# A decoder stack in fp32: weights repacked by the host, and the first tile's GpSimd and VectorE work in another order

## The chip, the cores and the metric

The kernel runs on one core of one Trainium2 chip. The metric is the device time of one execution in microseconds (us), lower is better. Before the change three executions took 3156.26, 3157.49 and 3159.41 us, a median of 3157.49 us. The engines in what follows: TensorE (PE; PEld is its weight load), VectorE (DVE), ScalarE (ACT), GpSimd (POOL), and SyncE (SP), which here only issues DMAs.

## The reference, cut to what matters

A stream x of 16 sequences of 128 tokens with 256 features passes three blocks, each on a normalised x and added to it. The change touches the first, a stack of 8 layers of linear attention and a feed-forward part.

```python
x = x + _L0_attn_ref(_layernorm(x, axis=-1), Wq, bq, Wk, bk, Wv, bv, Wo, bo, ln1_s, ln1_b, W1, b1, W2, b2, ln2_s, ln2_b)
x = x + _L0_xattn_ref(_layernorm(x, axis=-1), ctx_512, ...)
x = x + _L0_ffn_ref(_layernorm(x, axis=-1), ...)

def _L0_attn_ref(x, ...):                      # B, H, D, K, F = (8, 16, 256, 64, 1024)
    for i in range(B):
        residual = x
        Q = _feature_map(jnp.einsum('nsd,hdk->nshk', x, Wq[i]) + bq[i])      # elu(.) + 1
        Kf = _feature_map(jnp.einsum('nsd,hdk->nshk', x, Wk[i]) + bk[i])
        V = jnp.einsum('nsd,hdk->nshk', x, Wv[i]) + bv[i]
        KV = jnp.sum(Kf * V, axis=1)
        sumK = jnp.sum(Kf, axis=1)
        Z = 1.0 / (Q * sumK[:, None] + 1e-06)
        att = (Q * KV[:, None] * Z).reshape(n, s, H * K)
        y = jax.nn.gelu(att @ Wo[i] + bo[i])
        x = _layer_norm(y + residual, ln1_s[i], ln1_b[i])
        residual = x
        h = jax.nn.gelu(x @ W1[i] + b1[i])
        h = jax.nn.gelu(h @ W2[i] + b2[i])
        x = _layer_norm(h + residual, ln2_s[i], ln2_b[i])
    return x
```

## The kernel before, in words

The 16 sequences are four tiles of four sequences (512 tokens); x stays in SBUF as X. A layer's 16 heads are eight chunks of two heads, worked on in four pairs of chunks, p = 0 to 3. The stack is written as slots: slot(l, t) does the late parts of tile t (output projection, feed-forward) beside the projections and the attention of tile t+1. slot(0, -1) is the opening: only the four pairs of tile 0, with nothing else for TensorE to do. slot(0, 0) and slot(0, 1) follow, and then a loop over the layers. Each engine runs its own list of instructions in the order written, and semaphores join them. There is no scheduler.

**Weights.** An fp32 product is made of three fp32r products, so each weight is split into a high and a low part on GpSimd: `split_piece` waits for the piece in one of three STAGE buffers (`staged`), makes the high part (L262) and the low part (L264), and counts it in `w_lo`. A layer has 12 pieces: eight of 768 columns (Wk, Wv, Wq of two heads, 384 KB) and four of 512 columns (W1, 256 KB). SyncE loads piece k once `w_lo` says that piece k-3 is split. TensorE's pair p of tile 0 waits for `w_lo` of 2p+2 pieces.

**The input's norm.** For tile t, VectorE makes the statistics (L787, L791), GpSimd the rstd (L269, L271), VectorE the normed X (L779, four instructions, counted in `x0`). For tile 0, TensorE transposes X into PSUM (L375), ScalarE rounds it to XTHI (L550), and VectorE makes the remainder XTLO (L692). Only then can the projections start.

**One pair.** TensorE makes K, Q and V of two chunks, 36 matmuls (L341 to L343). ScalarE clips K (L505) and Q (L513) and takes Exp of both at once (L517). VectorE: `features` (L635, then L641 for K and L645 for Q, which read and free the PSUM banks that TensorE's next pair waits for), `sums_of` (L655, L660), `denominators` (L667, L669, L673, L676, L679). ScalarE then inverts (`invert`, L525 and L527), and VectorE's `newton` (L685, L687) corrects the inverse. ScalarE's `weigh` (L540) makes the attention from it. ScalarE's own order in slot(0, -1) puts `invert` of pair p-1 between the clips of K and of Q of pair p; the inversion of pair 2 stands behind the Exp of pair 3. EX and INV have two buffers each, so pair p+2 waits for pair p.

VectorE's order before: all statistics and all four norms of the input come first (L779 of tiles 1 to 3 before any `features`); GpSimd's order has rstd(t) in front of the pieces 2t and 2t+1. Tiles 1 to 3 of the normed input are first read in slots (0, -1) (tile 1, at its end), (0, 0) and (0, 1).

## Time and profile before

| what | value |
|---|---|
| median of three runs | 3157.49 us (3156.26 to 3159.41) |
| profiled execution, its time | 3159.65 us |
| its span, first to last instruction | 3158.1 us |
| mean granted TensorE clock | 0.963 |
| TensorE busy | 2933.1 us, 93% |
| VectorE busy | 2325.5 us, 74% |
| ScalarE, GpSimd busy | 1862.7 us, 921.5 us |
| DMA | 92.90 MB, mean 29 GB/s, 210193 packets, of them 147056 under 512 B |
| TensorE busy from 0 to 20, 20 to 45, 45 to 80 us | 1.97, 11.41, 25.88 us |
| TensorE busy from 200 to 300 us | 99.62 us |

Read the last two lines first: TensorE is close to full in the steady part of the stack and nearly empty in the first 80 us.

### The profile page before, as it was taken

Reading aid. Unit: us, or ns where it says so; the run is one execution under the profiler, and the core shown is the slowest. Engines: PE = TensorE matmul, PEld = TensorE weight load, DVE = VectorE, ACT = ScalarE, POOL = GpSimd, SP = SyncE. Lnnn points to the kernel's source line nnn. Section 1 sums busy time; section 2 is a strip of 40 time slices with the busy share of each in tenths; the row PEclk is TensorE's granted clock in tenths of the full one; section 3 lists DMA queues with packets and bytes.
Section 4 is the critical chain, followed back from the end, with each engine's and each line's share of the span. In section 5 each row is a group of like instructions: output and inputs, shape, how many; then the busy total and the mean of one; then the engine's idle time right before and its main releaser. Section 6 shows DMA issues by size and latency. Waiting matters only on the chain. (4 is left out here: it accounts for less than half of the span.)

```text
span 3158.1 us, 35422 instructions
## 1 busy us (share of the span) xinstructions
PE 2933.1 (93%) x11342; PEld 1989.8 (63%) x11343; DVE 2325.5 (74%) x3334; ACT 1862.7 (59%) x2796; POOL 921.5 (29%) x590
## 2 busy tenths in 40 slices
PE   4799999999999999999999999999999977997995
PEld 3566666666666665666566656665666635775563
DVE  7778888888887888887878788879787826763111
ACT  3666676667666776777677767776777713441121
POOL 5004231423152315231513151315131133333002
PEclk8899999999999999999999999999999987996998
DMA  5001101110111001100110011001100008000012
GB/s 129 1 1 23 26 8 32 27 27 6 30 27 27 12 25 27 27 17 19 26 27 17 19 26 27 17 19 26 28 17 4 1 3 269 0 0 24 12 45 77
DMA packets 210193, 92.90 MB, mean 29 GB/s; under 512 B 147056, under 2 KB 203632, under 8 KB 210000
## 3 DMA queue, kind: packets, MB, share of 16 engines
q1 hardware_dynamic: 207360, 83.30, 10.2%
q0 software_dynamic: 2640, 7.21, 0.7%
q8 instruction: 99, 1.62, 0.2%
q14 instruction: 94, 0.77, 0.1%
HBM read 80.24 MB, written 10.22 MB: 29 GB/s over the span
## 5 line engine op out<-in xcount | busy, mean ns | idle before, releaser
L341 PE MATMUL PS<-XTHI,WHI 128*128 128x512 f32 x1536 | 655.5, 427 | 60.8 <-DVE EX L641 41.5
L342 PE MATMUL PS<-XTLO,WHI 128*128 128x512 f32 x1536 | 614.1, 400 | 0.0
L343 PE MATMUL PS<-XTHI,WLO 128*128 128x512 f32 x1536 | 613.6, 399 | 0.0
L269 POOL TENSOR_TENSOR RSTD<-MV,EPS 128x4 f32<-128x4 f32 x68 | 41.1, 605 | 1537.7 <-DVE MV L713 1529.8
L391 PE MATMUL Y<-H,W2S 128*128 128x512 f32 x1024 | 458.2, 596 | 2.7 <-DVE R L703 2.7
L391 PE MATMUL Y<-ATT,WO 128*128 128x512 f32 x1024 | 451.7, 594 | 4.1 <-ACT ATT L540 2.7
L540 ACT ACTIVATE ATT<-INV,CC,CE 128x128 f32<-128x128 f32 x1024 | 424.9, 481 | 3.7 <-DVE INV L687 3.7
L341 PEld LDWEIGHTS PS<-XTHI,WHI 128*128 128x128 f32 x1536 | 294.5, 192 | 153.6 <-issue 64.6
L505 ACT ACTIVATE EX<-PS,BNEG 128x512 f32<-128x512 f32 x256 | 169.8, 686 | 309.9 <-PE PS L343 307.6
L342 PEld LDWEIGHTS PS<-XTLO,WHI 128*128 128x128 f32 x1536 | 294.8, 192 | 83.6 <-issue 20.3
L343 PEld LDWEIGHTS PS<-XTHI,WLO 128*128 128x128 f32 x1536 | 294.0, 191 | 70.0
L391 PEld LDWEIGHTS Y<-ATT,WO 128*128 128x128 f32 x1024 | 194.7, 190 | 226.2 <-issue 215.2
L391 PEld LDWEIGHTS Y<-H,W2S 128*128 128x128 f32 x1024 | 192.9, 191 | 210.9 <-issue 202.5
L660 DVE TENSOR_REDUCE SUMS<-EX 128x16 f32<-128x2048 f32 x128 | 292.4, 2284 | 3.3
L635 DVE TENSOR_SCALAR EX<-EX 128x2048 f32<-128x2048 f32 x128 | 224.2, 1752 | 43.1 <-ACT EX L517 43.0
L517 ACT ACTIVATE EX<-EX 128x2048 f32<-128x2048 f32 x128 | 245.3, 1917 | 4.1
L673 DVE TENSOR_TENSOR EX<-EX,ES 128x1024 f32<-128x1024 f32 x128 | 234.2, 1830 | 5.5
L685 DVE TENSOR_TENSOR EX<-EX,INV 128x1024 f32<-128x1024 f32 x128 | 164.8, 1287 | 90.5 <-ACT INV L527 90.2
L566 ACT ACTIVATE H<-PS,B 128x512 f32<-128x512 f32 x256 | 176.7, 690 | 79.7 <-PE PS L343 79.7
L341 PE MATMUL PS<-X1HI,W1HI 128*128 128x512 f32 x512 | 206.2, 403 | 0.1
L342 PE MATMUL PS<-X1LO,W1HI 128*128 128x512 f32 x512 | 203.1, 397 | 0.0
L703 DVE TENSOR_TENSOR R<-Y,R 128x1024 f32<-128x1024 f32 x32 | 39.2, 1225 | 222.3 <-PE Y L384 222.3
(180 smaller groups left out, 4823.9 us busy)
## 6 DMA issues: line engine op xcount, KB each, us to landing
STAGE<-L_attn_Wk SPq DMA_DIRECT2D x128, 64.0 KB, 2.1
STAGE<-L_attn_Wv SPq DMA_DIRECT2D x128, 64.0 KB, 2.1
STAGE<-L_attn_Wq SPq DMA_DIRECT2D x128, 64.0 KB, 2.1
WO<-L_attn_Wo SPq DMA_DIRECT2D x8, 1024.0 KB, 5.5
W2S<-L_attn_W SPq DMA_DIRECT2D x8, 1024.0 KB, 5.6
STAGE<-L_attn_W SPq DMA_DIRECT2D x64, 128.0 KB, 3.7
WGU<-L_ffn_r_gate SPq DMA_DIRECT2D x8, 512.0 KB, 10.2
WGU<-L_ffn_r_up SPq DMA_DIRECT2D x8, 512.0 KB, 9.5
```

The source lines that it names most:

```text
L341: nc.tensor.matmul(out, whi[:, kc, :], xhi[:, kc, :], start=(kc == 0), stop=False)
L342: nc.tensor.matmul(out, whi[:, kc, :], xlo[:, kc, :], start=False, stop=False)
L343: ins = nc.tensor.matmul(out, wlo[:, kc, :], xhi[:, kc, :], start=False, stop=(kc == KD - 1))
L391: ins = nc.tensor.matmul(Yfm[:, m, :], w[:, c, m * P:(m + 1) * P], src[:, c, :], start=(c == 0), stop=(c == HC - 1))
L505: nc.scalar.activation(EX[:, b, 2 + i, :], PS[:, KB + i, :], ACT.Relu, scale=-1.0, bias=BNEG[:, 0, 2 * p + i:2 * p + i + 1])
L517: nc.scalar.activation(EX[:, b, 2:6, :], EX[:, b, 2:6, :], ACT.Exp, scale=-1.0).then_inc(ex, 1)
L540: ins = nc.scalar.activation(ATT[:, 2 * p + i, ss], INV[:, b, i, ss], ACT.Identity, scale=CE[:, b, k:k + 1], bias=CC[:, b, k:k + 1])
L566: nc.scalar.activation(H[:, m, :], PS[:, QB + m % 4, :], ACT.Gelu_apprx_tanh, bias=B1[:, m:m + 1]).then_inc(h_act, 1)
L635: nc.vector.tensor_scalar(EX[:, b, 2:6, :], EX[:, b, 2:6, :], -1.0, 1.0, ALU.add, ALU.add).then_inc(snap, 1)
L660: nc.vector.tensor_reduce(SUMS[:, b, :], by_seq(EX[:, b, 0:4, :]), AX.X, ALU.add).then_inc(sums, 1)
L673: nc.vector.tensor_tensor(q, q, spread(ES[:, b, :], SEQ), ALU.add).then_inc(denom, 1)
L685: nc.vector.tensor_tensor(EX[:, b, 4:6, :], EX[:, b, 4:6, :], INV[:, b, :, :], ALU.mult).then_inc(residue, 1)
```

## The change

Host side: a function `packed` rearranges the stack's weights before launch, so that each SBUF tile or staged piece is one run of memory per partition in DRAM. Kernel side, the loads become one DMA each: a piece of Wk, Wv and Wq is one DMA with rows of 3 KB in place of six DMAs with rows of 256 B; a W1 piece one in place of two; the K, V and Q biases of half a layer one in place of three. Wo, W2 and the biases bo, b1, b2 keep their one DMA each, from the new layout. The semaphore counts follow. The splits stay the same.

In the opening, VectorE's order changes: XTLO of tile 0 comes right behind the norm of tile 0, and the norms of tiles 1, 2 and 3 move behind `denominators` of pairs 0, 1 and 2, in front of `newton`. `slot(0, -1)` is written out as a loop, in which every pair ends with its own `newton` before the next pair's `features`; before, `features` of pair 3 stood in front of `newton` of pair 2. GpSimd makes the rstd of tiles 1 to 3 together in front of piece 2, and waits for the normed X of tile 0 (`x0`) before it splits piece 0.

```diff
         def piece_incs(k):
-            return 16 * (3 * KD if k < HC else 2)
+            return 16
...
                 if k < HC:
-                    for m, w in enumerate((Wk, Wv, Wq)):
-                        dst = STAGE[:, s, m * KD * P:(m + 1) * KD * P]
-                        for kc in range(KD):
-                            src = w[layer, 2 * k:2 * k + 2, kc * P:(kc + 1) * P, :].rearrange("h p k -> p h k")
-                            sp.dma_start(dst[:, kc * P:(kc + 1) * P].rearrange("p (h k) -> p h k", h=2),
-                                         src).then_inc(staged[s], 16)
+                    sp.dma_start(STAGE[:, s, :], Wkvq[layer, k, :, :]).then_inc(staged[s], 16)
                 else:
...
+                    sp.dma_start(STAGE[:, s, 0:2 * KD * P], W1[layer, k - HC, :, :]).then_inc(staged[s], 16)
...
             def load_fm(dst, b, layer, done):
-                sp.dma_start(dst[:, :], b[layer, :].rearrange("(c p) -> p c", p=P),
-                             allow_slow_non_contiguous=True).then_inc(done, 16)
+                sp.dma_start(dst[:, :], b[layer, :, :]).then_inc(done, 16)
...
             for k in range(HC):
-                if k % 2 == 0:
-                    t = k // 2
-                    bs = slice(t * TS, (t + 1) * TS)
-                    rstd(RSTD0[:, bs], MV0[:, bs, 1], EPS0, mv0, 2 * t + 2, r0, t + 1)
+                if k == 0 or k == 2:
+                    for t in range(TILES)[:1] if k == 0 else range(1, TILES):
+                        bs = slice(t * TS, (t + 1) * TS)
+                        rstd(RSTD0[:, bs], MV0[:, bs, 1], EPS0, mv0, 2 * t + 2, r0, t + 1)
+                if k == 0:
+
+                    pool.wait_ge(x0, 1)
                 split_piece(0, k, True)
...
             input_statistics(0)
             norm_input(0)
+            input_lo(0)
             input_statistics(1)
-            input_lo(0)
             input_statistics(2)
             input_statistics(3)
-            for t in range(1, TILES):
-                norm_input(t)
-            slot(0, -1)
+            for p in range(PAIRS):
+                features(0, 0, p)
+                sums_of(0, 0, p)
+                denominators(0, 0, p)
+                if p < TILES - 1:
+                    norm_input(p + 1)
+                if p < PAIRS - 1:
+                    newton(0, 0, p)
+            input_lo(1)
             slot(0, 0)
```

VectorE at the start, before: BN_STATS and BN_AGGR are the statistics, `X<-X,MV,RSTD` the norm, and the last row the first instruction of pair 0.

```order
L779 TENSOR_SCALAR X<-X,MV,RSTD 128x256 x4
L787 BN_STATS ST<-X 128x6 x4
L791 BN_AGGR MV<-ST 128x2 x4
L692 TENSOR_TENSOR XTLO<-PS,XTHI 128x1024
L787 BN_STATS ST<-X 128x6 x4
L791 BN_AGGR MV<-ST 128x2 x4
L787 BN_STATS ST<-X 128x6 x4
L791 BN_AGGR MV<-ST 128x2 x4
L779 TENSOR_SCALAR X<-X,MV,RSTD 128x256 x12
L635 TENSOR_SCALAR EX<-EX 128x2048
```

VectorE at the start in the changed kernel (its line numbers are lower by ten: L769 is L779 before, L682 is L692, L625 is L635):

```order
L769 TENSOR_SCALAR X<-X,MV,RSTD 128x256 x4
L682 TENSOR_TENSOR XTLO<-PS,XTHI 128x1024
L777 BN_STATS ST<-X 128x6 x4
L781 BN_AGGR MV<-ST 128x2 x4
L777 BN_STATS ST<-X 128x6 x4
L781 BN_AGGR MV<-ST 128x2 x4
L777 BN_STATS ST<-X 128x6 x4
L781 BN_AGGR MV<-ST 128x2 x4
L625 TENSOR_SCALAR EX<-EX 128x2048
```

The twelve norm instructions of tiles 1 to 3 are gone from the front of pair 0, and XTLO stands ahead of the statistics of tile 1.

VectorE from the end of pair 0 to the start of pair 1, before: L660 is the reduce of `sums_of`, L667 to L679 are `denominators`, L685 and L687 are `newton`.

```order
L660 TENSOR_REDUCE SUMS<-EX 128x16
L667 TENSOR_SCALAR SUMS<-SUMS 128x8
L669 RECIPROCAL ES<-SUMS 128x8
L673 TENSOR_TENSOR EX<-EX,ES 128x1024
L676 SCALAR_TENSOR_TENSOR CC<-SUMS,ES 128x8
L679 TENSOR_TENSOR CE<-CC,ES 128x8
L685 TENSOR_TENSOR EX<-EX,INV 128x1024
L687 SCALAR_TENSOR_TENSOR INV<-EX,INV 128x1024
L635 TENSOR_SCALAR EX<-EX 128x2048
```

The same place in the changed kernel:

```order
L650 TENSOR_REDUCE SUMS<-EX 128x16
L657 TENSOR_SCALAR SUMS<-SUMS 128x8
L659 RECIPROCAL ES<-SUMS 128x8
L663 TENSOR_TENSOR EX<-EX,ES 128x1024
L666 SCALAR_TENSOR_TENSOR CC<-SUMS,ES 128x8
L669 TENSOR_TENSOR CE<-CC,ES 128x8
L769 TENSOR_SCALAR X<-X,MV,RSTD 128x256 x4
L675 TENSOR_TENSOR EX<-EX,INV 128x1024
L677 SCALAR_TENSOR_TENSOR INV<-EX,INV 128x1024
L625 TENSOR_SCALAR EX<-EX 128x2048
```

Four norm instructions (L769) stand between `denominators` and `newton`; four more each stand at that place of pairs 1 and 2.

GpSimd up to piece 3 before, where `WHI` and `WLO` are the two halves of one piece's split and `RSTD` the rstd of one tile:

```order
L271 TENSOR_TENSOR RSTD<-RSTD,HALF 128x4
L262 TENSOR_TENSOR WHI<-STAGE,ONE 128x768
L264 TENSOR_TENSOR WLO<-STAGE,WHI 128x768
L262 TENSOR_TENSOR WHI<-STAGE,ONE 128x768
L264 TENSOR_TENSOR WLO<-STAGE,WHI 128x768
L269 TENSOR_TENSOR RSTD<-MV,EPS 128x4
L271 TENSOR_TENSOR RSTD<-RSTD,HALF 128x4
L262 TENSOR_TENSOR WHI<-STAGE,ONE 128x768
L264 TENSOR_TENSOR WLO<-STAGE,WHI 128x768
```

And in the changed kernel:

```order
L251 TENSOR_TENSOR WLO<-STAGE,WHI 128x768
L256 TENSOR_TENSOR RSTD<-MV,EPS 128x4
L258 TENSOR_TENSOR RSTD<-RSTD,HALF 128x4
L256 TENSOR_TENSOR RSTD<-MV,EPS 128x4
L258 TENSOR_TENSOR RSTD<-RSTD,HALF 128x4
L256 TENSOR_TENSOR RSTD<-MV,EPS 128x4
L258 TENSOR_TENSOR RSTD<-RSTD,HALF 128x4
L249 TENSOR_TENSOR WHI<-STAGE,ONE 128x768
```

Three rstds stand ahead of piece 2, and none later: the pieces 2 to 11 follow one another.

## Rows read from the trace of the kernel before

**Rows 1.** The page's busy times, then the waits from 0 to 200 us.

```profile
PE 2933.1 (93%) x11342; PEld 1989.8 (63%) x11343; DVE 2325.5 (74%) x3334; ACT 1862.7 (59%) x2796; POOL 921.5 (29%) x590
...
PE PS L341 <- DVE EX L641: 26.7, 4, 13.8
```

**Rows 2.** The tile STAGE from 200 to 2500 us: waits for it.

```profile
  PE PS L343: 7.1, 7
```

**Rows 3.** Timeline, 7 to 25 us: start, us, engine, instruction, [idle before].

```profile
9.03 1.46 POOL L262 TENSOR_TENSOR WHI<-STAGE,ONE 128x768 fp32r<-128x768 f32 x1
9.07 4.09 DVE L779 TENSOR_SCALAR X<-X,MV,RSTD 128x256 f32<-128x256 f32 x4 [1.51 <-POOL RSTD L271]
...
15.22 1.01 ACT L550 CAST XTHI<-PS 128x1024 fp32r<-128x1024 f32 x1 [11.80 <-PE PS L375]
...
17.57 1.40 DVE L787 BATCH_NORM_STATS2 ST<-X 128x6 f32<-128x256 f32 x4 [4.41 <-DMA X<-x]
...
19.30 1.19 DVE L692 TENSOR_TENSOR XTLO<-PS,XTHI 128x1024 fp32r<-128x1024 f32 x1
...
20.60 0.77 PE L341 MATMUL PS<-XTHI,WHI 128*128 128x512 f32 x1 [5.41 <-DVE XTLO L692]
20.73 1.47 POOL L262 TENSOR_TENSOR WHI<-STAGE,ONE 128x768 fp32r<-128x768 f32 x1
...
24.05 1.52 POOL L262 TENSOR_TENSOR WHI<-STAGE,ONE 128x768 fp32r<-128x768 f32 x1
```

**Rows 4.** Line L779 from 9 to 14 us: ns min/median/max.

```profile
L779 DVE TENSOR_SCALAR X<-X,MV,RSTD x4: 400/984/1952, 9.1 to 12.8; 128x256 f32<-128x256 f32 x4
```

**Rows 5.** Timeline, 28 to 32 us.

```profile
28.84 6.82 DVE L779 TENSOR_SCALAR X<-X,MV,RSTD 128x256 f32<-128x256 f32 x4 [0.90 <-POOL RSTD L271]
...
29.97 1.92 ACT L517 ACTIVATE EX<-EX 128x2048 f32<-128x2048 f32 x1
```

**Rows 6.** Timeline, 43 to 61 us, VectorE alone.

```profile
43.54 1.21 DVE L635 TENSOR_SCALAR EX<-EX 128x2048 f32<-128x2048 f32 x1
...
48.94 2.29 DVE L660 TENSOR_REDUCE SUMS<-EX 128x16 f32<-128x2048 f32 x1
...
51.78 1.23 DVE L673 TENSOR_TENSOR EX<-EX,ES 128x1024 f32<-128x1024 f32 x1
52.92 1.00 DVE L676 SCALAR_TENSOR_TENSOR CC<-SUMS,ES 128x8 f32<-128x8 f32 x1
...
55.22 1.23 DVE L685 TENSOR_TENSOR EX<-EX,INV 128x1024 f32<-128x1024 f32 x1 [1.10 <-ACT INV L527]
56.48 1.95 DVE L687 SCALAR_TENSOR_TENSOR INV<-EX,INV 128x1024 f32<-128x1024 f32 x1
58.35 2.28 DVE L635 TENSOR_SCALAR EX<-EX 128x2048 f32<-128x2048 f32 x1
```

**Rows 7.** Timeline, 52 to 58 us, GpSimd alone.

```profile
52.10 1.80 POOL L262 TENSOR_TENSOR W1HI<-STAGE,ONE 128x512 fp32r<-128x512 f32 x1 [8.63 <-DMA STAGE<-L_attn_W]
53.98 1.31 POOL L264 TENSOR_TENSOR W1LO<-STAGE,W1HI 128x512 fp32r<-128x512 f32 x1
```

**Rows 8.** Timeline of SyncE's DMA issues; then all packets from 32 to 56 us.

```profile
35.16 0.47 SPq L192 DMA_DIRECT2D WO<-L_attn_Wo  x1
...
DMA packets 7510, 3.83 MB, mean 159 GB/s; under 512 B 3412, under 2 KB 7508, under 8 KB 7508
```

**Rows 9.** Timeline, 84 to 99 us, pair 3 and the start of slot (0, 0).

```profile
84.89 1.23 DVE L635 TENSOR_SCALAR EX<-EX 128x2048 f32<-128x2048 f32 x1 [1.00 <-ACT EX L517]
...
85.83 1.06 ACT L527 ACTIVATE INV<-INV 128x1024 f32<-128x1024 f32 x1
...
96.87 1.22 DVE L692 TENSOR_TENSOR XTLO<-PS,XTHI 128x1024 fp32r<-128x1024 f32 x1
...
98.19 0.77 PE L341 MATMUL PS<-XTHI,WHI 128*128 128x512 f32 x1 [9.09 <-issue]
```

**Rows 10.** Windows: length, busy (instructions) of PE, PEld, DVE, ACT, POOL; PEclk, DMA.

```profile
80.00:120.00 40.00, 28.27 (x103) 19.90 (x102) 28.42 (x37) 24.44 (x37) 0.00 (x0) 0.83 0.00 1
```

More of the change, by code:

```diff
@@ L162, in load_piece @@
                 if k < HC:
[L163 to L175 removed]
+                    sp.dma_start(STAGE[:, s, :], Wkvq[layer, k, :, :]).then_inc(staged[s], 16)
+                else:
+                    sp.dma_start(STAGE[:, s, 0:2 * KD * P], W1[layer, k - HC, :, :]).then_inc(staged[s], 16)
             def load_ba(layer, half):
                 cs = slice(half * HC // 2, (half + 1) * HC // 2)
[L179 to L181 removed]
+                sp.dma_start(BA[:, :, cs], bkvq[layer, half, :, :, :]).then_inc(ba_in[half], 16)
             def load_ln(dst, scale, bias, layer, done):
@@ L187, in load_fm @@
             def load_fm(dst, b, layer, done):
-                sp.dma_start(dst[:, :], b[layer, :].rearrange("(c p) -> p c", p=P),
-                             allow_slow_non_contiguous=True).then_inc(done, 16)
+                sp.dma_start(dst[:, :], b[layer, :, :]).then_inc(done, 16)
             def load_wide(dst, w, layer, done):
-                sp.dma_start(dst[:, :, :], w[layer, :, :].rearrange("(c p) n -> p c n", p=P)).then_inc(done, 16)
+                sp.dma_start(dst[:, :, :], w[layer, :, :, :]).then_inc(done, 16)
             def layer_loads(l):
@@ L494, in clip_keys @@
                     cs = slice(2 * p, 2 * p + 4)
[L495 removed]
+                    act.wait_ge(ba_in[p // 2], (l + 1) * 16)
                     if at_least(l, t, 1):
@@ L1720, in decoder, with packed, by_side @@
             mixture(nc, X, ident, out, ffn)
+def packed(a, np):
+    out = {n: v for n, v in a.items() if n[:8] != "L0_attn_"}
+    def by_side(w, sizes):
+        return np.ascontiguousarray(w.reshape(sizes[0]).transpose(sizes[1]).reshape(sizes[2]))
+    L = LAYERS
+    w = [a["L0_attn_W" + n].reshape(L, HC, 2, KD, P, HK) for n in "kvq"]
+    out["L0_attn_Wkvq"] = by_side(np.stack(w, 2), ((L, HC, 3, 2, KD, P, HK), (0, 1, 5, 2, 4, 3, 6), (L, HC, P, PIECE)))
+    b = [a["L0_attn_b" + n].reshape(L, 2, HC // 2, P) for n in "kvq"]
+    out["L0_attn_bkvq"] = by_side(np.stack(b, 2), ((L, 2, 3, HC // 2, P), (0, 1, 4, 2, 3), (L, 2, P, 3, HC // 2)))
+    out["L0_attn_W1"] = by_side(a["L0_attn_W1"], ((L, KD, P, HC // 2, 2, P), (0, 3, 2, 4, 1, 5), (L, HC // 2, P, 2 * KD * P)))
+    for n in ("Wo", "W2"):
+        out["L0_attn_" + n] = by_side(a["L0_attn_" + n], ((L, HC, P, D), (0, 2, 1, 3), (L, P, HC, D)))
+    for n, c in (("bo", KD), ("b1", HC), ("b2", KD)):
+        out["L0_attn_" + n] = by_side(a["L0_attn_" + n], ((L, c, P), (0, 2, 1), (L, P, c)))
+    for n in ("ln1_s", "ln1_b", "ln2_s", "ln2_b"):
+        out["L0_attn_" + n] = a["L0_attn_" + n]
+    return out
 def kernel(**inputs):
@@ L1730 @@
               for name, a in inputs.items()}
+    arrays = packed(arrays, np)
     aps = {name: nc.dram_tensor(name, a.shape, mybir.dt.from_np(a.dtype), kind="ExternalInput").ap()
```

14 lines of the change are left out of this document (2 added, 12 removed).

## The prediction

> **What bounds the kernel now.** First the page's busy times and the waits from 0 to 200 us [rows 1]. TensorE is busy 2933.1 of 3158.1 us, and its largest wait of the first 200 us has one place: 13.8 of the 26.7 us that it waited for VectorE's L641. Then the loop over the layers. Of its STAGE buffers the one wait that shows is for TensorE to free the weights, 7.1 us in 7 [rows 2], and none is for a DMA. So in the loop the weights are there before GpSimd wants them, and whatever the new loads save there is worth nothing. What is left is the opening, and there I read the timeline.
>
> TensorE starts the projections at 20.60, when XTLO is done [rows 3]. XTLO itself ran at 19.30 though its input was ready at 16.23 (15.22 + 1.01): VectorE stood in its list at the statistics of tile 1, whose X landed at 17.57. ScalarE's Exp of pair 0 ends at 31.89 (29.97 + 1.92) [rows 5], but `features` starts at 43.54 [rows 6], since the norms of tiles 2 and 3 stand in front. One set of four takes 6.82 us [rows 5] where a lone instruction takes 0.40 [rows 4]: VectorE gets one instruction in per instruction of GpSimd. So 11.65 us are lost between Exp and `features`, and TensorE, whose PSUM banks are freed by `features`, waits with it.
>
> How VectorE and GpSimd exclude each other carries most of the sum. Row L676 took 1.00 us at 52.92 to the end of GpSimd's high part (52.10 + 1.80); that one in its turn took 1.80, since it had waited for L673 to end at 53.01 [rows 6, 7]. VectorE's L687 (1.95), and L635 (2.28 against 1.21), show the same. XTLO and the reduce L660 have no second length beside GpSimd in these rows, and I take the same of L641, L645 and L655, which read PSUM as XTLO does. The Trainium skill, "SBUF — State Buffer", section "Who interferes with whom", says that an instruction with two SBUF inputs or in a two-port mode and a GpSimd instruction block each other whole. If the port were shared in bandwidth instead, step 3 below would cost next to nothing and the light rival would be the forecast; by that rule, it would not.
>
> **The change part by part**, against the profiled execution (3159.65 us, its span 3158.1 plus 1.5, and 2.2 above the median of 3157.49). I give times as they would stand in a trace.
>
> 1. Start. The rstd of tile 0 ends at 9.03 as now. GpSimd now waits for the norm, so it runs alone: four at a pitch of 0.34 (0.40 each, overlapping; the pitch is an estimate from the length and the 0.06 that follows it) end at about 10.45, not 13.16. That brings the transposes, XTHI (16.23 now, so 13.5) and XTLO (14.8) 2.7 us and more forward. GpSimd's first two pieces start at 10.5 instead of 9.03, and a piece takes 3.32 (20.73 to 24.05) [rows 3], so w_lo reaches 2 at 10.5 + 6.7 = 17.2. Their data must be there: six issues a piece become one, and X and three pieces are requested in about 4 us. TensorE starts at 17.25 instead of 20.60: 3.35 us.
>
> 2. `features` of pair 0. Exp ended 11.3 us after TensorE's start (31.89 - 20.60), so it ends at 28.55, and VectorE is free: three statistics of about 1.75 from 14.8 end at 20.1. `features` can start at 28.55 instead of 43.54: 15.0 us.
>
> 3. What comes back. GpSimd used to be idle from 43.5 to 52.10, the 8.63 us of waiting for W1 [rows 7]; pair 0 ran in that hole. Now GpSimd makes three rstds and starts piece 2 at about 21.6. Six pieces of 3.32 last to 41.5 even undisturbed, then W1's four pieces of 2.4 (1.04 when not blocked, 1.31, and gaps). Pair 0 meets that train. Walking down VectorE's list: L635 meets a high part begun at 28.45, waits to 29.95 and ends at 31.05. L641 to L660 are not touched and take 6.4 (51.23 - 43.54 less the 1.25 of L635) to 37.45. L667 waits for a high part (37.85), L673 for the low part behind it, done 40.75; L676 and L679 for another high part, 42.5. The first instruction of the norm of tile 1 waits for the last low part of the pieces, 44.1, and ends at 44.45. Whether the other three cost 1.05 or one W1 instruction each (1.2) hangs on when W1's first piece lands. Wo was requested at 35.16 [rows 8], and W1 was there at 52.10, 17 us later, behind 2.6 MB and the biases in 4-byte elements. Now Wo goes at 33.4, when piece 7 may be loaded (w_lo of 5), and without the single elements: an estimate of 11 to 13 us puts it at 44.5 to 46.5. I take 45.4. Then the norm ends at 45.5, L685 waits for one W1 instruction (47.7), L687 and the next L635 for one each, and this L635, of pair 1, ends at 52.25. It ended at 60.63 before. So from 15.0 ahead VectorE falls to 8.4 ahead: step 3 costs 6.6. Behind it GpSimd is through with W1 at about 58.4, before L667 of pair 1, and the norm of tile 2 stands where VectorE waits for ScalarE's inversion anyway. The bounds: 0, without any blocking, even a gain of 1.1, since L635, L676 and L687 were blocked before; and 9.1, if W1 is there at 44.1 and all three norm instructions, L685, L687 and L635 take a W1 instruction each.
>
> 4. Pair 3. `features` stood ahead of `newton` of pair 2 and started at 84.89. Now `newton` comes first and needs ScalarE's inversion, which stands behind the Exp of pair 3 and ends at 86.89 (85.83 + 1.06) [rows 9]. From there VectorE's list holds the same instructions as before up to XTLO of tile 1, 13.2 us (84.89 to 98.09), with no wait among them, and TensorE starts slot (0, 0) behind that XTLO, 0.1 us later (98.19). So 2.0 us are lost. The norm of tile 3 (1.4) hides in the wait. Bounds: 0, if the inversion came in time, and 2.4, were `newton` wholly added.
>
> 5. The rest. The loads in the loop: 0 [rows 2], below nothing excluded and above nothing too, since none is waited for. After slot (0, 0) has begun, each engine's list is unchanged, so what is gained there stays.
>
> Sum: -15.0 + 6.6 + 2.0 = -6.4 us, a span of 3151.7 and 3151.1 against the median. I say **3151.3 us**.
>
> The Trainium skill, "DMA: Bandwidth & Descriptors", section "Rules for kernel authors", says that a last dimension that isn't contiguous costs one descriptor an element. The trace agrees in that 3412 of 7510 packets were under 512 B between 32 and 56 us [rows 8]; some 1536 of them would be these biases. By that rule alone the queue in front of W1 empties sooner than I took it, which makes the dense train below likelier and not the forecast better.
>
> **The rivals.**
>
> Dense train. W1 lands before GpSimd is free at 44.1, or X so late (as at 17.57 now) that the whole train moves back and covers more of pair 1. GpSimd then has no hole, and VectorE gets one instruction in per GpSimd instruction through norm and `newton`. For: four norm instructions took 6.82 in such a train [rows 5]. Against: W1 took 17 us to come before. Step 3 costs 9.1 instead of 6.6: -3.9, 3153.6 us. With a late X 1 to 2 more.
>
> Light train. VectorE reaches its blocked instructions in GpSimd's gaps, or W1 comes after 47. For: a tie of 0.1 us decides at 28.5, worth 1.3, and L676 found GpSimd's gap between 53.90 and 53.98 [rows 6, 7]. Against: GpSimd is busy without a hole until 44. With W1 late -7.9 (3149.6); with no blocking at all -15.0 - 1.1 + 2.0 = -14.1 (3143.4).
>
> Given back later. TensorE in slots (0, 0) to (0, 2) waits for something not moved by the opening, so part of the gain ends in a wait there. For: no row that I have. Against: Wo was requested at 35.16 [rows 8] and is used after 98. It would be worth 2 to 6 us of the gain: 3153 to 3157.
>
> Slower, by TensorE's clock. From 80 to 120 us the granted clock is 0.83 at 28.27 us of work [rows 10], so part of slot (0, 0) runs at the lower of its two levels after stretches of waiting, as the start does too. If the moved waits left it all at 1.2 GHz, this work would take (0.83 - 0.5) / 0.5 of 28.27 longer, 18.7 us, and the time would be 3169.8 us. It ends on the slow side once more than 12.7 us are lost so, that is if that stretch falls below about 0.61. For: TensorE still waits between pairs. Against: it waits less than before ahead of pair 1 and of slot (0, 0).
>
> That the change doesn't do what it says: only if TensorE's pair 1 waits for the pieces 2 and 3, split by 28.4, needed at 31.8. Three us of delay in X would start it, and each more costs its length; it is part of the dense train.
>
> **How the numbers follow.** Forecast case (W1 within some 1.5 us of GpSimd's being free, -4.8 to -8.4): 0.43. Dense train 0.23, light train 0.22, given back 0.06, slower by the clock 0.06. A change of this kernel's time by under 0.2%, 6.3 us, can hardly be told from none. The forecast case straddles that bound, half on each side. Faster: 0.21 + 0.22 = 0.43. Within: 0.22 + 0.23 + 0.06 = 0.51. Slower: 0.06. The range from 3145.5 to 3157.0 leaves out the no-blocking end and the clock, and holds the others; the forecast case alone spans 3149.1 to 3152.7.
>
> **What the changed profile would show.** Step 1: the four norms in under 1.6 us, TensorE's L341 at 17.3, waiting for GpSimd's `w_lo` and no longer for XTLO. Step 2: L635 of pair 0 at 28.6. Step 3: L673, L676 and the norm of tile 1 stretched to GpSimd's pitch, and L635 of pair 1 done at 52.3; W1's high part waiting little or not at all for its DMA. Step 4: VectorE waiting for ScalarE's L527 ahead of `newton` of pair 2, about 2 us. Step 5: TensorE's slot (0, 0) starts near 91.8, and from there each engine's later rows lie 6.4 us earlier. I am wrong if pair 1's L635 ends outside 50 to 55.5, if slot (0, 0) starts as forecast and the span doesn't follow, or if the stretches after 200 us have other busy shares.

## The result and the profile after

The changed kernel takes **3142.58 us** (median of five runs, 3137.61 to 3144.07), the kernel before 3157.49 us (3155.34 to 3159.41): a ratio of 0.995, with an interval of 0.9936 to 0.9965. The gain of 14.9 us is more than twice the 6.4 us forecast, and the time lies below the range given (3145.5 to 3157.0). The profiled execution is the 3142.58 us one, with a span of 3140.5 us.

The page of the changed kernel, which answers [rows 1]:

```profile
PE 2925.5 (93%) x11342; PEld 1984.7 (63%) x11343; DVE 2305.1 (73%) x3334; ACT 1863.0 (59%) x2796; POOL 922.0 (29%) x590
...
DMA packets 59658, 92.82 MB, mean 30 GB/s; under 512 B 14960, under 2 KB 38768, under 8 KB 57424
```

The same bytes go in 59658 packets, where it was 210193. The waits from 0 to 200 us (total, times, longest):

```profile
PE PS L331 <- DVE EX L631: 22.5, 4, 9.5
```

TensorE's longest wait for `features` fell from 13.8 to 9.5 us. The waits for STAGE buffers between 200 and 2500 us still name no DMA [rows 2]:

```profile
  PE PS L333: 12.2, 7
```

The timeline of the start (start, us, engine, instruction, idle before and its releaser), against [rows 3]:

```profile
9.02 1.38 DVE L769 TENSOR_SCALAR X<-X,MV,RSTD 128x256 f32<-128x256 f32 x4 [1.51 <-POOL RSTD L258]
...
12.46 1.01 ACT L540 CAST XTHI<-PS 128x1024 fp32r<-128x1024 f32 x1 [9.03 <-PE PS L365]
...
13.50 1.23 DVE L682 TENSOR_TENSOR XTLO<-PS,XTHI 128x1024 fp32r<-128x1024 f32 x1 [3.10 <-ACT XTHI L540]
...
17.28 0.77 PE L331 MATMUL PS<-XTHI,WHI 128*128 128x512 f32 x1 [4.86 <-POOL WLO L251]
...
26.43 1.92 ACT L507 ACTIVATE EX<-EX 128x2048 f32<-128x2048 f32 x1
...
28.38 2.08 DVE L625 TENSOR_SCALAR EX<-EX 128x2048 f32<-128x2048 f32 x1 [8.52 <-ACT EX L507]
```

VectorE from `denominators` of pair 0 on, against [rows 6]:

```profile
37.48 2.45 DVE L663 TENSOR_TENSOR EX<-EX,ES 128x1024 f32<-128x1024 f32 x1
39.86 1.43 DVE L666 SCALAR_TENSOR_TENSOR CC<-SUMS,ES 128x8 f32<-128x8 f32 x1
...
41.40 2.88 DVE L769 TENSOR_SCALAR X<-X,MV,RSTD 128x256 f32<-128x256 f32 x4
44.20 1.21 DVE L675 TENSOR_TENSOR EX<-EX,INV 128x1024 f32<-128x1024 f32 x1
45.45 1.23 DVE L677 SCALAR_TENSOR_TENSOR INV<-EX,INV 128x1024 f32<-128x1024 f32 x1
46.59 2.06 DVE L625 TENSOR_SCALAR EX<-EX 128x2048 f32<-128x2048 f32 x1
...
55.88 2.09 DVE L663 TENSOR_TENSOR EX<-EX,ES 128x1024 f32<-128x1024 f32 x1
```

GpSimd beside it, against [rows 7]:

```profile
41.34 1.82 POOL L251 TENSOR_TENSOR WLO<-STAGE,WHI 128x768 fp32r<-128x768 f32 x1
45.97 1.61 POOL L249 TENSOR_TENSOR W1HI<-STAGE,ONE 128x512 fp32r<-128x512 f32 x1 [2.80 <-DMA STAGE<-L_attn_W]
```

GpSimd is through with the pieces at 43.16 and has nothing until W1's piece is there at 45.97. Into that hole fall the end of the norm and both halves of `newton`: L675 and L677 take 1.21 and 1.23 us, their length with no GpSimd beside them.

Pair 3 and the start of slot (0, 0), against [rows 9]:

```profile
65.51 0.76 PE L331 MATMUL PS<-XTHI,WHI 128*128 128x512 f32 x1 [5.46 <-DVE EX L631]
...
77.36 1.06 ACT L517 ACTIVATE INV<-INV 128x1024 f32<-128x1024 f32 x1
78.45 1.23 DVE L675 TENSOR_TENSOR EX<-EX,INV 128x1024 f32<-128x1024 f32 x1 [4.12 <-ACT INV L517]
...
90.44 1.22 DVE L682 TENSOR_TENSOR XTLO<-PS,XTHI 128x1024 fp32r<-128x1024 f32 x1
...
91.75 0.77 PE L331 MATMUL PS<-XTHI,WHI 128*128 128x512 f32 x1 [6.21 <-issue]
```

Slot (0, 0) starts at 91.75, 6.44 us ahead of 98.19. The window after it has the clock it had [rows 10]:

```profile
80.00:120.00 40.00, 30.21 (x104) 20.77 (x105) 28.41 (x36) 21.69 (x32) 0.00 (x0) 0.83 0.00 1
```

**Where the rest came from.** As a mark in every slot I take the first multiply of the first layer norm on GpSimd (one a tile, 32 in all). Its first stands at 148.96 before and 142.21 after, its last at 2550.51 and 2536.73: 6.75 us ahead at the loop's start, 13.78 at its end. So the loop over the layers, where I had said nothing changes, gave 7.0 us. What follows the last mark (607.6 and 603.8 us) isn't different in kind: over all profiles here it is 598 to 613 us. By slots, 5.5 of the 7.0 us lie in six of them, those that begin with the loop's return. One row differs there on every return: the pause of ScalarE ahead of its table load. Kernel before, its waits, then the timeline of the fourth return:

```profile
ACT L546 <- issue: 15.2, 6, 2.7
```

```profile
1507.01 1.28 ACT L546 ACT_TABLE_LOAD   x1 [2.46 <-issue]
...
1510.49 1.23 DVE L685 TENSOR_TENSOR EX<-EX,INV 128x1024 f32<-128x1024 f32 x1 [3.05 <-ACT INV L527]
```

Changed kernel, the same two views:

```profile
ACT L536 <- issue: 9.4, 6, 1.8
```

```profile
1499.16 1.28 ACT L536 ACT_TABLE_LOAD   x1 [1.45 <-issue]
...
1502.64 1.23 DVE L675 TENSOR_TENSOR EX<-EX,INV 128x1024 f32<-128x1024 f32 x1 [2.04 <-ACT INV L517]
```

The table load waits for nothing that the profile shows, but comes 1.0 us sooner. The inversion behind it does too, and VectorE's `newton` waits 2.04 us for it instead of 3.05. The norm and the next burst of splits stand behind `newton`.

TensorE in three of these slots (from:to, length, busy, granted clock), one of the kernel before:

```profile
1477.37:1558.55 81.18, 77.91 (x289) 0.98 0.10 21
```

Two of the changed kernel:

```profile
1156.33:1236.92 80.59, 77.83 (x289) 0.98 0.07 21
1470.59:1549.90 79.31, 77.83 (x296) 1.00 0.07 22
```

TensorE's work is 77.8 to 77.9 us in each. The slot takes 81.05 to 81.33 us in all six returns before, and after 80.6 to 80.9 in four and 79.2 to 79.3 in two.

TensorE's wait for `features` in the first and in the last of these three slots (total, times, longest):

```profile
PE PS L341 <- DVE EX L641: 2.3, 1, 2.3
```

```profile
PE PS L331 <- DVE EX L631: 0.4, 1, 0.4
```

In the middle one it is 2.2 us. So an inversion that comes 1.0 us sooner takes either some 0.4 us off the slot or, where this wait shrinks to 0.4 us, 1.9 us.

One thing in the code fits. A wait for the biases needs its value in a register: (l+1)·48 before, for three DMAs, and (l+1)·16 after, which is also what the loop's waits for `bo`, `b1` and `b2` compare with, so ScalarE's compiled loop has one register instruction less.

### The profile page after: what moved, and what is told of

The parts are those of the page before. It is cut to its first block and busy times, and to the rows that moved or that the text cites. A ratio compares the mean times of both kernels' runs of the same rounds, so it can differ in the third digit from the quotient of the medians.

```text
span 3140.5 us, 34598 instructions
## 1 busy us (share of the span) xinstructions
PE 2925.5 (93%) x11342; PEld 1984.7 (63%) x11343; DVE 2305.1 (73%) x3334; ACT 1863.0 (59%) x2796; POOL 922.0 (29%) x590
## 2 busy tenths in 40 slices
DMA packets 59658, 92.82 MB, mean 30 GB/s; under 512 B 14960, under 2 KB 38768, under 8 KB 57424
## 5 line engine op out<-in xcount | busy, mean ns | idle before, releaser
L625 DVE TENSOR_SCALAR EX<-EX 128x2048 f32<-128x2048 f32 x128 | 224.0, 1750 | 49.8 <-ACT EX L507 49.8
L663 DVE TENSOR_TENSOR EX<-EX,ES 128x1024 f32<-128x1024 f32 x128 | 236.2, 1845 | 5.5
L675 DVE TENSOR_TENSOR EX<-EX,INV 128x1024 f32<-128x1024 f32 x128 | 165.0, 1289 | 96.9 <-ACT INV L517 96.7
L556 ACT ACTIVATE H<-PS,B 128x512 f32<-128x512 f32 x256 | 176.9, 691 | 79.5 <-PE PS L333 79.4
L333 PE MATMUL PS<-X1HI,W1LO 128*128 128x512 f32 x512 | 202.8, 396 | 0.0
```

What stands on the lines that cost most here:

```text
L333: ins = nc.tensor.matmul(out, wlo[:, kc, :], xhi[:, kc, :], start=False, stop=(kc == KD - 1))
L556: nc.scalar.activation(H[:, m, :], PS[:, QB + m % 4, :], ACT.Gelu_apprx_tanh, bias=B1[:, m:m + 1]).then_inc(h_act, 1)
L625: nc.vector.tensor_scalar(EX[:, b, 2:6, :], EX[:, b, 2:6, :], -1.0, 1.0, ALU.add, ALU.add).then_inc(snap, 1)
L663: nc.vector.tensor_tensor(q, q, spread(ES[:, b, :], SEQ), ALU.add).then_inc(denom, 1)
L675: nc.vector.tensor_tensor(EX[:, b, 4:6, :], EX[:, b, 4:6, :], INV[:, b, :, :], ALU.mult).then_inc(residue, 1)
```

## The experiments

Theories for the loop. **Place**: ScalarE's one instruction less puts the loop at another place in its list, and the stall at the return depends on that place. **Body**: the count of instructions in the loop decides. **Loads**: fewer DMAs or packets, or SyncE's shorter list, free the loop. For the opening: what each part of the order is worth.

"Slot" is TensorE's start of slot (0, 0); "stall" ScalarE's six pauses; "loop" the time from the first mark to the last. Before: 98.19, 2.5 to 2.7, 2401.6. Changed: 91.75, 1.4 to 1.8, 2394.5. Differences in medians are against the kernel before on the same chip, which took 3160.22 (beside e1 to e4), 3160.27 (e5 to e8), 3162.21 (e9 to e11), 3161.49 (e12 to e14) and 3160.38 us (e15 to e18).

| run | median | ratio (interval) | slot | stall | loop |
|---|---|---|---|---|---|
| e1_opening_only | 3155.50 | 0.9988 (0.9978–0.9998) | 95.66 | 2.5–2.8 | 2400.6 |
| e2_loads_only | 3152.12 | 0.9971 (0.9961–0.9981) | 99.46 | 1.4–1.9 | 2399.6 |
| e3_six_dmas | 3149.84 | 0.9973 (0.9962–0.9984) | 93.92 | 2.5–2.7 | 2401.1 |
| e4_pair3_order | 3140.10 | 0.9942 (0.9925–0.9958) | 89.73 | 1.4–1.6 | 2388.9 |
| e5_no_x0_wait | 3148.15 | 0.9961 (0.9949–0.9974) | 94.63 | 1.4–1.7 | 2396.1 |
| e6_best | 3140.20 | 0.9938 (0.9923–0.9954) | 87.47 | 1.5–1.8 | 2395.5 |
| e7_sync_long | 3140.34 | 0.9944 (0.9929–0.9958) | 92.21 | 1.4–1.7 | 2394.7 |
| e8_scalar_plus_one | 3150.74 | 0.9973 (0.9963–0.9982) | 90.72 | 2.5–2.7 | 2402.2 |
| e9_bias_only | 3154.67 | 0.9978 (0.9967–0.9989) | 99.51 | 1.4–1.8 | 2389.4 |
| e10_before_loop | 3151.62 | 0.9968 (0.9956–0.9979) | 90.60 | 2.5–2.6 | 2400.6 |
| e11_body_plus_four | 3152.11 | 0.9953 (0.9937–0.9970) | 91.27 | 1.5–1.8 | 2398.8 |
| e12_three_ahead | 3139.64 | 0.9930 (0.9915–0.9944) | 91.81 | 1.5–1.8 | 2391.7 |
| e13_changed_again | 3143.56 | 0.9949 (0.9937–0.9961) | 89.67 | 1.4–1.8 | 2395.5 |
| e14_best_again | 3137.73 | 0.9932 (0.9918–0.9946) | 87.17 | 1.4–1.8 | 2389.2 |
| e15_before_plus_one | 3147.15 | 0.9951 (0.9935–0.9968) | 99.86 | 1.5–1.8 | 2394.6 |
| e16_plus_five | 3130.99 (one run) | | 90.49 | 1.4–1.6 | 2387.2 |
| e17_plus_nine | 3147.20 (one run) | | 90.69 | 1.4–1.7 | 2392.7 |
| e18_plus_seventeen | 3144.01 (one run) | | 90.19 | 1.5–1.8 | 2395.5 |

### The two halves of the change, and the number of DMAs

**e1_opening_only**: the loads of before with the new order on VectorE and GpSimd.

```diff
+                if k == 0:
+                    pool.wait_ge(x0, 1)
...
-            slot(0, -1)
+            for p in range(PAIRS):
```

> Only the new order on VectorE and GpSimd in the opening; all loads, layouts and ScalarE's waits as before the change. Theory O (the order carries the opening, the loads carry the loop): TensorE starts slot (0, 0) between 91 and 94 us instead of 98.19, and in the loop ScalarE keeps its stall of 2.5 us ahead of the table load at each of the six returns of the loop, so the later slots keep their old lengths (81.1 us for the one with the first split burst) and the time is 3157.5 - 4 to 6.5 = 3151 to 3153.5. Rival L (the order carries all, and what happens in the loop is a matter of phase): the time is near the changed kernel's 3142.6, with ScalarE's stall near 1.5 us.

The order alone starts slot (0, 0) 2.5 us sooner, less than I had expected (91 to 94 us), and the time is 4.7 us lower in the median; the stall and the loop are those of before. TensorE starts as early as in the changed kernel, and the loss comes later. The timeline of e1:

```profile
17.40 0.76 PE L343 MATMUL PS<-XTHI,WHI 128*128 128x512 f32 x1 [4.85 <-POOL WLO L264]
...
54.02 1.04 POOL L262 TENSOR_TENSOR W1HI<-STAGE,ONE 128x512 fp32r<-128x512 f32 x1 [8.39 <-DMA STAGE<-L_attn_W]
...
60.64 4.06 DVE L781 TENSOR_SCALAR X<-X,MV,RSTD 128x256 f32<-128x256 f32 x4
```

With the old loads W1 lands at 54.02, not 45.97, and its splits meet the rows of pair 1: the norm there takes 4.06 us, where the changed kernel took 1.38.

**e2_loads_only**: the new loads, the old order.

```diff
-            for p in range(PAIRS):
...
+            for t in range(1, TILES):
+                norm_input(t)
+            slot(0, -1)
```

> Only the new layout and the single DMAs; the order on VectorE and GpSimd as before. Theory O: X and the pieces land sooner, so that the statistics of tile 1 no longer hold up XTLO; the norms of tiles 2 and 3 still stand ahead of pair 0, so slot (0, 0) starts 2 to 4 us earlier than 98.19; in the loop ScalarE's stall is 1.4 to 1.8 us instead of 2.5 and the slot with the first burst 80.6 instead of 81.1: 3 us over the loop, and up to 4 more by TensorE's clock. Time 3147 to 3152. Rival L: the loop is as before, 3154 to 3156.

The opening gains nothing (99.46; the order of before stood at 98.19, 99.51 and 99.86 in three profiles), where I had expected 2 to 4 us, yet the median is 8.1 us lower, and the stall is the short one. The profiled execution is the slowest of e2's twelve, and its loop is only 2.0 us shorter than before. So the short stall came with the loads' part of the change.

**e3_six_dmas**: the changed kernel with six DMAs for each piece, two for W1's and three for the biases, from the new layout.

```diff
-                    sp.dma_start(STAGE[:, s, :], Wkvq[layer, k, :, :]).then_inc(staged[s], 16)
+                    for j in range(6):
+                        cols = slice(j * P, (j + 1) * P)
+                        sp.dma_start(STAGE[:, s, cols], Wkvq[layer, k, :, cols]).then_inc(staged[s], 16)
...
-                    act.wait_ge(ba_in[p // 2], (l + 1) * 16)
+                    act.wait_ge(ba_in[p // 2], (l + 1) * 48)
```

> The changed kernel with its packed layout, but each piece of Wk, Wv and Wq loaded by six DMAs (rows of 512 B), a W1 piece by two, the biases of half a layer by three, as many issues as before the change, and ScalarE waiting for 48 as before. Theory O1 (the loop is shorter since SyncE and ScalarE have fewer instructions in its body): ScalarE's stall at the loop's return is back to 2.5 us and the time is 3146 to 3150. Rival O2 (rows of 256 B, now gone, disturbed something): the stall stays at 1.4 to 1.8 and the time at 3141 to 3145. The opening loses up to 1 us in either case.

The stall and the loop of before are back, and the opening loses some 3 us (93.92), where I had expected 1 at most: W1 lands at 51.51. Which of the edits brought the stall back e7 and e8 tell.

### Whose list it is

**e7_sync_long** keeps only the six and the two DMAs of e3: SyncE's list is long again, ScalarE's stays short.

> The changed kernel with six DMAs for a weight piece and two for a W1 piece, so that SyncE's list is as long as in e3, but the biases in one DMA and ScalarE's list as in the changed kernel. Theory S (SyncE's longer list, or its DMAs, delays ScalarE at the loop's return): stall 2.5 us as in e3, time about e3's 3150. Theory A (ScalarE's own list is what counts, one register instruction shorter): stall 1.4 to 1.7 and slots with the first split burst of 79.2 to 80.8, time 3142 to 3146.

**e8_scalar_plus_one** keeps only the three bias DMAs and the wait for 48.

```diff
-                sp.dma_start(BA[:, :, cs], bkvq[layer, half, :, :, :]).then_inc(ba_in[half], 16)
+                for m in range(3):
+                    sp.dma_start(BA[:, m, cs], bkvq[layer, half, :, m, :]).then_inc(ba_in[half], 16)
...
-                    act.wait_ge(ba_in[p // 2], (l + 1) * 16)
+                    act.wait_ge(ba_in[p // 2], (l + 1) * 48)
```

> The changed kernel with the biases of half a layer in three DMAs and ScalarE waiting for 48 a layer, which makes one register instruction more in ScalarE's loop, as before the change; the pieces keep their one DMA. Theory A: stall 2.5 us, the slot with the first split burst back at 81.1, time 3147 to 3151. Theory S: stall 1.4 to 1.7, time near 3143.

With all 96 pieces fetched in small DMAs e7 is as fast as the changed kernel (19.9 us ahead of before in the median, 17.7 by its ratio). With one register instruction more on ScalarE e8 loses 10.4 us to e7 in the median, on the same chip, with the same order in the opening; the loops of the two profiles differ by 7.5. The waits of e8:

```profile
ACT L537 <- issue: 15.6, 6, 2.7
```

So the theory of the loads, as a matter of DMAs, packets or SyncE's list, falls.

**e9_bias_only**: the kernel before with the packed biases alone, so that ScalarE waits for 16.

```diff
-                    act.wait_ge(ba_in[p // 2], (l + 1) * 48)
+                    act.wait_ge(ba_in[p // 2], (l + 1) * 16)
```

> The kernel before the change with one thing of it: the K, V and Q biases of half a layer come in one DMA from the packed layout and ScalarE waits for 16 a layer, which takes one register instruction out of ScalarE's loop (980 instead of 981 instructions). Weights, their DMAs and the opening are as before. Theory A (that instruction carries the gain in the loop): ScalarE's stall falls from 2.5 to 1.4 to 1.7 us, the slots with the first split burst from 81.1 to 79.2 to 80.8, the stretch from the first to the last tile from 2401.5 to about 2395, slot (0, 0) starts where it did (98.2), and the time is 6 to 8 us under the kernel before. Rival: the weights' layout or DMAs are needed too, and the time is within 2 us of before.

The time falls by 7.5 us, as expected, with an opening as late as before (99.51) and the short stall.

### Place or body

**e10_before_loop** adds one instruction ahead of the loop to the changed kernel, a wait that is long fulfilled, and leaves the body alone.

```diff
             attention_tables()
+            act.wait_ge(x0, 1)
             input_hi(0)
```

> The changed kernel with one more instruction on ScalarE ahead of its loop (a wait that is always met), the loop's body as in the changed kernel. Theory length (the body's length counts, 453 against 454 instructions): stall 1.4 to 1.7, time near 3142. Theory place (where the body or its end lies in ScalarE's list counts; its end is now where it was before the change): stall 2.5, time near 3150. Nothing else moves.

The waits of e10, then TensorE in the slot behind its fourth return:

```profile
ACT L536 <- issue: 15.1, 6, 2.6
```

```profile
1469.60:1550.74 81.14, 77.90 (x289) 0.98 0.07 21
```

The long stall is back with an unchanged body: body falls, place stands.

**e11_body_plus_four** adds two waits to ScalarE's slot in the loop, four instructions in all, and **e12_three_ahead** adds two such waits only in the written-out slots, three instructions ahead of the loop. The edit of e11:

```diff
+                if type(l) is not int:
+                    act.wait_ge(x0, TILES)
+                    act.wait_ge(mv0, 2 * TILES)
```

> The changed kernel with four more instructions in ScalarE's loop (waits that are always met, one in each slot). If the stall grows with each instruction it is over 4 us; if it has two levels, it is 2.5 as with one more; if one more mattered by an odd or even place, it is back at 1.5. The time follows: about 3155, 3150 or 3142.

> The changed kernel with three more instructions on ScalarE ahead of its loop (waits that are always met), body as in the changed kernel; one more gave a stall of 2.5 us, four more in the body gave 1.6. If the stall is high for every list that is longer than a limit, it is 2.5 here. If it depends on the place in some small block, it is 2.5 or 1.5, and with e10 and e11 at one and four more it says that more than one place of four is bad or that only one is. The time is 3150 or 3142.

Both have the short stall. A longer list or a later place isn't slow in itself. e11's median of 3152.11 us looks long for that, though by its ratio it is 14.9 us below before; its loop is the second longest of the short-stall kernels.

**e15_before_plus_one** puts e10's line into the kernel before. **e16_plus_five**, **e17_plus_nine** and **e18_plus_seventeen** put 5, 9 and 17 of them into the changed kernel. Their expectations count a place for each wait, and that is wrong: the compiler puts two such waits into one instruction, as in e11 and e12. The pages count 34601, 34603 and 34607 instructions against the changed kernel's 34598, so these loops end at +3, +5 and +9.

> The kernel before with one instruction more in ScalarE's list ahead of the loop (a wait for the norm of tile 0 in front of its first rounding, which TensorE's transposes wait for anyway). Counted from the changed kernel, whose loop ends at place 0, the loops with the long stall at the return all ended at +1 (before, and the experiments with one instruction more), those with the short one at 0, +3 and +4. If +1 is a bad place, this loop ends at +2 and the stall is short: 1.4 to 1.8 us instead of 2.5 to 2.7, the time 6 to 8 us below the kernel before, slot (0, 0) still at 98.2. If it is the count of instructions in the loop's body (one more than in the changed kernel), the stall stays at 2.5 to 2.7 and the time at the kernel before's.

> The changed kernel with five such waits ahead of the loop: it ends at +5. If the bad place comes back every 4 instructions, the stall is 2.5 to 2.7 us; if it comes back every 8 or 16 or never, 1.4 to 1.8.

> The same with nine waits, +9. Long (2.5 to 2.7 us) if the bad place comes back every 8 (or every 4) instructions, short (1.4 to 1.8) if every 16 or never.

> The same with seventeen waits, +17. Long (2.5 to 2.7 us) if the bad place comes back every 16 instructions (or every 8 or 4); short if it comes back at another pitch or never.

The kernel before gets faster by one added instruction, 13.2 us in the median, nearly what the whole change brought. I had expected 6 to 8, and the loops of the two profiles differ by 6.9; the rest is not explained. The waits of e15, then TensorE in a slot behind a return:

```profile
ACT L546 <- issue: 9.7, 6, 1.8
```

```profile
851.40:930.58 79.18, 77.84 (x296) 1.00 0.11 22
```

Counted from where the loop of the changed kernel ends in ScalarE's list, five kernels end at +1 (before, e1, e3, e8, e10), and they alone have the long stall: 2.5 to 2.8 us in all 30 returns. At 0, +2, +3, +4, +5 and +9 it is 1.4 to 1.9, in all 90. On three of the chips both kinds of kernel ran, so it isn't the chip. Nor does the place of the loop's start alone decide it: e10 and e15 both start theirs one later than the changed kernel, and only e10 has the long stall. The place +5 (e17) says that the bad one doesn't come back every 4 instructions, and +9 (e18) that it doesn't every 8. Whether it comes back every 16 was not tested, since no kernel ends at +17. What makes it bad stays open.

The five loops take 2400.6 to 2402.2 us, the fifteen others 2387.2 to 2399.6, on average 2393.6. That is 7.6 us less, for six stalls of 1.0. Between the same marks the 30 return slots with the long stall take 81.0 to 81.4 us. Of the 90 with the short one 50 take 80.6 to 81.1 and 40 take 79.2 to 79.4, the ones in which TensorE waits 0.4 to 0.6 us for `features` and not 2.2 or more. The mean is 1.1 us lower, 6.5 for six slots. The rest, 1.2, lies in the slots behind them, which take 80.3 or 81.6 to 81.9 us. So one stall fixes one slot only loosely. How many of a kernel's six returns fall into the lowest group, one in e2 and e11, two in the changed kernel, five in e16, makes most of the spread among the fifteen, and e16's 3130.99 us is one such run.

### The opening

**e4_pair3_order** puts `newton` of pair 2 behind `features` of pair 3, as before.

```diff
                 features(0, 0, p)
+                if p == 3:
+                    newton(0, 0, 2)
...
-                if p < PAIRS - 1:
+                if p < 2:
```

> The changed kernel, but features of pair 3 stand again in front of newton of pair 2. In the changed kernel VectorE waits 4.12 us for ScalarE's inversion ahead of newton of pair 2. Theory W (that wait is wholly on the path to XTLO of tile 1): L625 of pair 3 starts at 76.4, right behind the Exp, XTLO ends 4.5 us earlier and slot (0, 0) starts at 87.3 instead of 91.75; the time falls by 4 to 4.5 us to 3138. Rival: another wait takes its place (TensorE's transposes, ScalarE's table load) and under 2 us are won, 3141 to 3143.

Slot (0, 0) starts at 89.73, 2.0 us sooner than in the changed kernel's profile. I had expected 4.5 (87.3). And the changed kernel itself starts it at 89.67 in e13, so this can't be told from the spread of the opening.

**e5_no_x0_wait** takes away GpSimd's wait for the normed X of tile 0.

```diff
-                if k == 0:
-
-                    pool.wait_ge(x0, 1)
```

> The changed kernel without GpSimd's wait for the normed X of tile 0 ahead of piece 0. Theory O: GpSimd starts at 9.0 and blocks the four norm instructions again (4.1 us, X at 13.2), XTLO ends at 17.4 in place of 14.7, while w_lo of 2 comes at 15.8 in place of 17.2; TensorE starts at 17.4 to 17.6 instead of 17.28, so the wait is worth 0 to 0.3 us at the start. Rival: GpSimd's train ends 1.4 us earlier and VectorE's pair 0 gains it, slot (0, 0) at 90.3 instead of 91.75.

I had expected 0.3 us at most. The timeline of e5:

```profile
8.97 1.46 POOL L249 TENSOR_TENSOR WHI<-STAGE,ONE 128x768 fp32r<-128x768 f32 x1
9.01 6.79 DVE L766 TENSOR_SCALAR X<-X,MV,RSTD 128x256 f32<-128x256 f32 x4 [1.52 <-POOL RSTD L258]
...
12.26 1.51 POOL L249 TENSOR_TENSOR WHI<-STAGE,ONE 128x768 fp32r<-128x768 f32 x1
...
20.24 0.77 PE L328 MATMUL PS<-XTHI,WHI 128*128 128x512 f32 x1 [2.41 <-issue]
```

The piece behind the first now lands in time, so GpSimd has no hole, and the norm takes 6.79 us, where before it took 4.09 beside a late piece [rows 3]. TensorE starts at 20.24, not 17.28, and slot (0, 0) at 94.63. The wait is worth 3.0 us at TensorE's start. e2, which lacks it too, has the same 6.79 and 20.24: without the wait the new loads save next to nothing at the start against the 20.60 of before. What the wait is worth with the old loads was not tested. The halves don't add up for both reasons: the loads alone lose their gain to the longer norm, and the order alone (e1) meets a late W1.

**e6_best** has the order of e4, and the norm of tile 1 ahead of pair 0.

```diff
+            norm_input(1)
             for p in range(PAIRS):
...
-                if p < TILES - 1:
+                if 0 < p < TILES - 1:
```

> As e4 (features of pair 3 ahead of newton of pair 2), and the norm of tile 1 stands in front of pair 0, where VectorE is idle from 19.9 to 28.4 while GpSimd splits pieces 2 and 3. Theory W: the four instructions take 6.7 us there, done at 27.9, and pair 0 loses the 2.88 us that they took between its denominators and newton; newton then starts right behind ScalarE's inversion at 42.1 instead of 44.20. Slot (0, 0) starts 2 us earlier than in e4 (89.73), at 87.7, and the time is 1 to 3 us under e4's. Rival: the norm runs over 28.4 and gives the gain back, or TensorE at its lower clock sets pair 1; then it is equal to e4.

Slot (0, 0) starts at 87.47, as expected, but the time isn't the 1 to 3 us under e4's: the ratios are 0.9938 and 0.9942, the medians 3140.20 and 3140.10 us.

**e13_changed_again** and **e14_best_again** are the changed kernel and e6 once more, on one chip.

> The changed kernel itself, on the same chip as the next one. The stall is 1.4 to 1.8 and slot (0, 0) starts at 91.8 or, if TensorE has its full clock in pair 3, at 89.5 to 90.8. The time is 14 to 18 us under the kernel before.

> The version with the norm of tile 1 ahead of pair 0 and features of pair 3 ahead of newton of pair 2, on the same chip as the changed kernel. Slot (0, 0) starts at 87.5, 3 to 4.3 us earlier than there, and nothing of that is given back: the time is 3 to 4.5 us under the changed kernel's.

The timeline of VectorE in e14:

```profile
19.77 1.35 DVE L769 TENSOR_SCALAR X<-X,MV,RSTD 128x256 f32<-128x256 f32 x4
...
27.11 1.99 DVE L625 TENSOR_SCALAR EX<-EX 128x2048 f32<-128x2048 f32 x1 [6.00 <-ACT EX L507]
```

The norm of tile 1 runs in 1.35 us in VectorE's wait for the Exp (I had expected 6.7, in a train of splits; it met the rstds instead). Slot (0, 0) starts at 87.47 in e6 and 87.17 in e14. On one chip e14 takes 3137.73 us, the changed kernel 3143.56, the kernel before 3161.49. This version is clearly faster than the kernel before. Its 5.8 us on the changed one are not shown: the intervals of the two ratios overlap (0.9918 to 0.9946 and 0.9937 to 0.9961), and the loops of the two profiles, which the edit doesn't touch, differ by 6.3 us. Its opening does start slot (0, 0) 2.5 us sooner here.

## Why the prediction was wrong, step by step

1. **Start: right.** The four norm instructions take 1.38 us (forecast under 1.6), and TensorE starts at 17.28 (17.25), waiting for `w_lo`. e5 shows that without the added wait it would be 20.24.

2. **`features` of pair 0: right.** It starts at 28.38, against a forecast of 28.55.

3. **What comes back: mechanism right, size off.** L625 of pair 1 ends at 48.65, not 52.25, outside the 50 to 55.5 that I had set as a bound for the step. The term of 6.6 us measured 3.2: 15.16 ahead at pair 0 (28.38 against 43.54), 11.98 at the end of that row (48.65 against 60.63). GpSimd was through at 43.16 (forecast 44.1), W1 came at 45.97 (45.4). The hole of 2.8 us, not 1.3, held the rest of the norm and `newton`. By the Trainium skill, "SBUF — State Buffer", section "Who interferes with whom", the block is an exclusive lock; the trace agrees in both directions, 6.79 us for four norm instructions beside an unbroken train (e5) and 1.21 us for L675 in the hole.

4. **Pair 3: right in form, but a loss ahead of it was missed.** From the end of ScalarE's inversion to XTLO's end it took 13.2 us, as forecast (78.45 to 91.66). But the inversion's end was only 8.5 us ahead of before (78.42 against 86.89), where pair 1 had been 12.0. Of this 1.1 went at L657 and L663 of pair 1 (0.45 and 2.09 us beside GpSimd, 0.17 and 1.23 before), since pair 2's L625 was 10.9 ahead. The other 2.4 went in TensorE's projections of pair 3. TensorE in pair 3 (stretch, length; the first busy time and the clock are TensorE's), before:

```profile
76.30:86.90 10.60, 8.61 (x36) 6.70 (x36) 9.32 (x14) 10.28 (x18) 0.00 (x0) 1.00 0.00 0
```

Changed:

```profile
65.50:78.50 13.00, 10.99 (x36) 8.44 (x36) 8.64 (x16) 10.46 (x18) 0.00 (x0) 0.80 0.00 0
```

The same 36 matmuls take 10.99 us at a granted clock of 0.80, where they took 8.61 at 1.00. TensorE had waited 5.46 us ahead of them, 3.38 before, and part of them ran at the lower of its two levels. That is the clock rival, at an eighth of its price (2.4 of 18.7 us) and at another place. In e13, the same kernel, it waited 4.32 us, the clock was 0.86, the busy time 10.18, and slot (0, 0) started at 89.67:

```profile
64.20:76.40 12.20, 10.18 (x36) 7.82 (x36) 8.66 (x16) 10.48 (x18) 0.00 (x0) 0.86 0.00 0
```

So the errors of 3 and 4 cancelled in this profile: the 6.44 us match the forecast by luck. Over nine profiles with the changed opening (the changed kernel twice, e8, e10, e11, e12, e16 to e18) it starts at 90.8 on average, over the three with the order and pieces of before at 99.2: 8.4 us.

5. **The loop: this step failed.** It said that the loads are worth 0 in the loop, "since none is waited for", and that "after slot (0, 0) has begun, each engine's list is unchanged". The first half holds: e7 fetches every piece in six DMAs and loses nothing. The second is false. The list that orders the rows of instructions was unchanged, but ScalarE's list with its register instructions was one shorter, and that moved the loop's end from the bad place. The term that I put at 0 measured 7.0 us between the two profiles, and 7.6 between the five loops that end there and the fifteen others. I had named the test (slot (0, 0) as forecast and the span not following), and this is what came about. With 0 in the loop the changed kernel would lie where e8 and e10 are, 9.5 and 10.6 us below before, at 3147 to 3148 us by the median of this case: in my range. The 7.0 to 7.6 us of the loop put it outside.

Behind it, the Trainium skill, "Runtime: NRT & Kernel Launch", section "Instruction fetch mechanics", says that a taken branch whose target lies outside the blocks that the engine holds waits for a fetch. That each return costs ScalarE 1.4 us or more while the profile names nothing would agree. It does not give the difference of 1.0 us between places one instruction apart. The pages' instruction packets of the second queue don't follow the stall either: 93 in e8 (long) and in e11 and e12 (short), 94 in e10 (long) and e15 (short), 87 in the changed kernel. It was not shown that the stall is a fetch.

**The rivals.** Dense train: no, GpSimd had a hole. Light train with W1 late (3149.6): nearest for step 3. Given back later: no. Slower by the clock: as said, 2.4 us in one pair. The no-blocking end (3143.4) comes near the 3142.58 us by number alone: L663 of pair 0 took 2.45 us beside GpSimd, 1.23 before. In the clock rival's working the stretch would have to fall to 0.57, not 0.61, to lose 12.7 us; it measured 0.83 again. None held a gain in the loop, and the lower end of the range rested on the opening alone.
